# Attention pass of a macaron block: a new order of all engines, 26 waits fewer a turn

## The reference

```python
x = x + 0.5 * ffn(layernorm(x))
x = x + attn(layernorm(x))
x = x + 0.5 * ffn(layernorm(x))
```

```python
q, k, v = x @ Wq, x @ Wk, x @ Wv            # q and k then have length 1 in each head
alpha, beta = sigmoid(x @ Wa + ba), sigmoid(x @ Wb + bb)
state = alpha * state + outer(k, beta * (v - k @ state))    # token by token, 32x32 a head
y = q @ state
out = (rmsnorm(y, g_norm) * silu(x @ Wg)) @ Wo
```

## Time and profile before

| | us |
|---|---|
| median of 3 runs | 2782.89 |
| lowest and highest | 2769.9, 2797.73 |
| the profiled execution | 2779.95 |
| its span on the core | 2777.7 |
| TensorE busy | 2591.8 (93%) |
| VectorE, ACT, GpSimd busy | 1857.1, 1043.4, 1326.3 |

### The profile page before, as it was taken

How to read it: one execution, slowest core, us unless ns; L and a number is a source line. 1 busy time by engine, 2 the same in 40 slices (tenths; PEclk the granted TensorE clock), 3 DMA queues, 4 the chain that set the end, 5 groups by cost and what they waited for, 6 DMA issues and landing times.

```text
span 2777.7 us, 117151 instructions
## 1 busy us (share of the span) xinstructions
PE 2591.8 (93%) x51052; PEld 1871.6 (67%) x51052; DVE 1857.1 (67%) x5306; ACT 1043.4 (38%) x1962; POOL 1326.3 (48%) x1767
## 2 busy tenths in 40 slices
PE   7999779999999999999999999999999999999768
PEld 6788456666666667766666667776666666776544
DVE  7778456766666767666666677666676667766726
ACT  5777323333333333333333333333333333333220
POOL 2222345554545555555555555555555455555510
PEclk9999999999999999999999999999999999999968
DMA  7342122222222222222222222222222222222178
GB/s 238 104 152 85 24 66 54 62 62 65 65 65 65 64 58 64 57 66 65 57 61 65 65 65 62 65 65 60 54 61 59 65 65 65 65 65 61 54 256 317
DMA packets 365965, 224.78 MB, mean 81 GB/s; under 512 B 277584, under 2 KB 294032, under 8 KB 365456
## 3 DMA queue, kind: packets, MB, share of 16 engines
q1 hardware_dynamic: 356240, 200.51, 25.8%
q10 hardware_dynamic: 9216, 16.78, 1.6%
HBM read 125.49 MB, written 74.97 MB: 72 GB/s over the span
## 4 chain that ended last, share of the span: by engine, by line
PE 84%; DVE 8%; issue 4%; ACT 1%; DMA 1%; POOL 1%; SPq 1%; DVEq 0%; ACTq 0%; POOLq 0%
PE psum L849 24%; PE psum L906 8%; PE psum L1048 8%; PE psum L1029 5%; PE psum L970 5%; PE psum L946 4%; PE psum L1069 4%; PE psum L1009 3%; PE psum L1016 3%; PE psum L690 3%; PE psum L753 3%; PE psum L989 2%; PE psum L836 1%; PE psum L927 1%; PE psum L1089 1%
## 5 line engine op out<-in xcount | busy, mean ns | idle before, releaser
L849 PE MATMUL psum<-w_all,xnT 128*128 128x512 f32 (+2 forms) x2048 | 740.2, 500 | 1.4 <-issue 0.7
L2020 POOL TENSOR_TENSOR sm<-sm,half 128x1 f32<-128x1 f32 (+1 forms) x384 | 530.1, 1381 | 247.0 <-ACT sm L1715 231.0
L849 PEld LDWEIGHTS psum<-w_all,xnT 128*128 128x128 f32 x2048 | 369.0, 191 | 201.8 <-issue 158.2
L2585 DVE TENSOR_TENSOR blk<-blk 128x30 f32<-128x30 f32 (+14 forms) x960 | 327.8, 341 | 33.0
L2583 DVE TENSOR_TENSOR blk<-blk 128x30 f32<-128x30 f32 (+14 forms) x960 | 318.2, 331 | 40.0 <-issue 14.3
L2052 POOL TENSOR_SCALAR sm<-sm 128x1 f32<-128x1 f32 x64 | 14.8, 231 | 625.3 <-DVE sm L2490 625.3
L906 PEld LDWEIGHTS psum<-xnT,w_all 128*128 128x128 f32 x2048 | 256.0, 197 | 42.1 <-issue 34.8
L906 PE MATMUL psum<-xnT,w_all 128*128 128x128 f32 x2048 | 277.2, 285 | 1.5 <-DVE pk L2570 1.5
L1048 PE MATMUL psum<-w_out,gate 128*128 128x512 f32 x512 | 258.4, 618 | 3.0 <-issue 2.0
L1029 PEld LDWEIGHTS psum<-qg,st 32*32 32x32 f32 x8192 | 133.6, 109 | 130.0 <-DVE st L2602 64.7
L2602 DVE STREAM_TRANSPOSE st<-psum 128x128 f32<-128x128 f32 x256 | 81.0, 316 | 189.8 <-PE psum L1029 188.6
(11 more groups left out here) (278 smaller groups left out, 4719.1 us busy)
## 6 DMA issues: line engine op xcount, KB each, us to landing
blk<-n_scratch SPq DMA_DIRECT2D x64, 512.0 KB, 4.4
xin<-in_L_attn_x_dram SPq DMA_DIRECT2D x96, 256.0 KB, 3.1
n_scratch<-nn SPq DMA_DIRECT2D x64, 256.0 KB, 3.4
xh<-xc SPq DMA_DIRECT2D x64, 256.0 KB, 2.3
e_scratch<-blk SPq DMA_DIRECT2D x32, 512.0 KB, 2.8
E<-e_scratch SPq DMA_DIRECT2D x64, 256.0 KB, 3.9
x_scratch<-xh SPq DMA_DIRECT2D x62, 256.0 KB, 2.2
rxn<-in_L_attn_x_dram SPq DMA_DIRECT2D x32, 256.0 KB, 2.9
```

The costliest lines, as they stand in the source:

```text
L849: last = mm(dst, xnT[b][:, k * P:(k + 1) * P], w_all[:, k * WK + at:k * WK + at + n], start=(k == 0), stop=(k == KC - 1))
L2020: return g.tensor_tensor(dst, a, half[:, 0:n], ALU.pow)
L2585: ins = tt(Y[:, 0:rows, s_ + 1:CH], Y[:, 0:rows, s_ + 1:CH], o, ALU.add)
```

## The change

The order of all five engines in the attention pass is another; so are the PSUM banks. Waits that another wait implies are left out (many `free` and `wait_ge` lines), on TensorE 828 waiting instructions in all: a turn now has 1527 weight loads, 1527 matmuls and 18 waits, 3072 instructions. The arithmetic is the same.

A turn of TensorE now begins with apply_uw(r, 0), which stood in the turn before as apply_uw(q, 0). The cut of a turn in the functions is thus another, and the functions of b = 0 that bore the argument q there bear r here.

```diff
-        va_at = [banks(1, 1), banks(4, 1)]
+        va_at = [banks(1, 1), banks(5, 1)]
...
-        cum_at = banks(1, 1)[:, 0:8 * H]
+        cum_at = banks(6, 1)[:, 0:8 * H]
         aT_at = banks(4, 1)[:, 0:P]
-        slot_at = banks(1, 1)
+        slot_at = banks(2, 1)
...
             def ffn(n):
                 pe.wait_ge(at_in, 16 * n)
-                free((n - 2, (T["qg"][1], nth(n - 2, 0))), (n - 1, (T["pt"][0], nth(n - 1, 0))))
-                free((n - 2, (T["qg"][1], nth(n - 2, 1))), (n - 1, (S["kn"], both(n - 1, 1))))
+                free((n - 2, (T["qg"][1], nth(n - 2, 1))), (n - 1, (T["pt"][0], nth(n - 1, 0))))
+                free((n - 3, (S["slc"], n - 3)), (n - 2, (S["x2"], both(n - 2, 0))), (n - 1, (S["x1"], both(n - 1, 1))))
...
             def cum(n):
-                pe.wait_ge(S["la"], n)
-                free((n - 2, (S["slc"], n - 2)), (n - 1, (S["x2"], both(n - 1, 0))), (n, (S["va"], both(n, 0))))
+                free((n - 1, (S["ysq"], both(n - 1, 0))), (n, (S["kn"], both(n, 0))))
...
                 if piece == 0:
                     pe.wait_ge(e_in[b], 16 * n)
-                    pe.wait_ge(S["va"], both(n, b))
-                    pe.wait_ge(S["vb"], both(n, b))
-                    pe.wait_ge(S["kp"], both(n, b))
...
             def step_sp(o, p, q, r, s):
                 store_second(r, 0)
                 hold(q, 0)
+                load_alpha(o)
                 store_second(r, 1)
-                load_first(p, 1)
+                load_first(o, 0)
                 store_alpha(s)
                 hold(q, 1)
                 inverse_out(q)
-                load_alpha(o)
+                load_first(o, 1)
                 inverse_in(q, 0)
                 inverse_in(q, 1)
-                load_first(o, 0)
```

More of the change, by code:

```diff
@@ L1091, in alpha_T @@
             def alpha_T(n):
-                pe.wait_ge(S["al"], both(n + NT, 1))
-                free((n + 3, (S["xnT"], both(n + 3, 0))), (n + 2, (T["pt"][1], nth(n + 2, 1))), (n, (S["top"], both(n + NT, 0))))
                 tr(aT_at, alpha[:, :], ident[:, :]).then_inc(aT_ps, 1)
             def last_pe():
+                apply_uw(NT - 2, 0, 0)
+                apply_uw(NT - 2, 0, 1)
+                apply_uw(NT - 2, 0, 2)
+                apply_uw(NT - 2, 0, 3)
+                proj_va(NT - 1, 1, 0)
+                apply_gy(NT - 2, 0, 0)
+                proj_va(NT - 1, 1, 1)
+                proj_k(NT - 1, 1, 0)
+                proj_k(NT - 1, 1, 1)
+                proj_k(NT - 1, 1, 2)
+                proj_k(NT - 1, 1, 3)
+                apply_gy(NT - 2, 0, 1)
+                gram(NT - 1, 0, 0)
+                apply_gy(NT - 2, 0, 2)
+                gram(NT - 1, 0, 1)
+                apply_gy(NT - 2, 0, 3)
+                proj_q(NT - 1, 1, 0)
+                proj_q(NT - 1, 1, 1)
+                proj_q(NT - 1, 1, 2)
+                proj_q(NT - 1, 1, 3)
+                chain(NT - 2, 0, 0)
+                dec(NT - 1, 0)
                 chain(NT - 2, 0, 1)
-                dec(NT - 1, 0)
+                gram(NT - 1, 0, 2)
                 chain(NT - 2, 0, 2)
+                dec(NT - 1, 1)
+                gram(NT - 1, 0, 3)
+                logits(NT - 3, 1)
                 chain(NT - 2, 0, 3)
-                gram(NT - 1, 0, 2)
-                gram(NT - 1, 0, 3)
-                dec(NT - 1, 1)
-                out_proj(NT - 2, 0, 0)
                 gram(NT - 1, 1, 0)
@@ L1333, in first_pe @@
                 gram(1, 1, 3)
+                cum(1)
                 proj_g(1, 1, 0)
                 proj_g(1, 1, 1)
+                proj_g(1, 0, 0)
+                ffn(2)
                 proj_g(1, 1, 2)
-                cum(1)
-                ffn(2)
-                proj_g(1, 0, 0)
                 proj_g(1, 0, 1)
@@ L1470, in first_pe @@
-                proj_q(3, 1, 2)
-                proj_q(3, 1, 3)
-                chain(2, 0, 0)
-                gram(3, 0, 0)
-                gram(3, 0, 1)
-            def step_pe(o, p, q, r, s):
+                proj_va(3, 0, 1)
+                qe_T(2, 0, 1)
+            def step_pe(o, p, q, r, s):
+                apply_uw(r, 0, 0)
+                apply_uw(r, 0, 1)
+                apply_uw(r, 0, 2)
+                apply_uw(r, 0, 3)
+                proj_va(q, 1, 0)
+                apply_gy(r, 0, 0)
+                proj_va(q, 1, 1)
+                proj_k(q, 1, 0)
+                proj_k(q, 1, 1)
+                proj_k(q, 1, 2)
+                proj_k(q, 1, 3)
+                apply_gy(r, 0, 1)
+                gram(q, 0, 0)
+                apply_gy(r, 0, 2)
+                gram(q, 0, 1)
+                apply_gy(r, 0, 3)
+                proj_q(q, 1, 0)
+                proj_q(q, 1, 1)
+                proj_q(q, 1, 2)
+                proj_q(q, 1, 3)
+                chain(r, 0, 0)
+                dec(q, 0)
@@ L1477, in step_pe @@
                 chain(r, 0, 1)
-                dec(q, 0)
+                gram(q, 0, 2)
                 chain(r, 0, 2)
+                dec(q, 1)
+                gram(q, 0, 3)
+                logits(s, 1)
                 chain(r, 0, 3)
-                gram(q, 0, 2)
-                gram(q, 0, 3)
-                dec(q, 1)
-                out_proj(r, 0, 0)
                 gram(q, 1, 0)
@@ L1565, in step_pe @@
-                proj_q(p, 1, 1)
-                proj_q(p, 1, 2)
-                proj_q(p, 1, 3)
-                chain(q, 0, 0)
-                gram(p, 0, 0)
-                gram(p, 0, 1)
+                proj_va(p, 0, 1)
+                qe_T(q, 0, 1)
             first_pe()
```

890 lines of the change are left out of this document (411 added, 479 removed).

## The result

The changed kernel takes 2711.4 us (median of 4 runs, 2706.17 to 2713.64) against 2779.59 for the kernel before in the same comparison: ratio 0.9739, 95% interval 0.9708 to 0.9769. It is **faster by 2.6%**; the forecast was 2791 us, no change. Its profiled execution took 2713.64 us.

What follows compares the result with a forecast made beforehand. TensorE, losing time at borders of 256-instruction groups, was taken as the bound. Work 68.8, waits 0.5, borders 3.4 and 0.2 made 72.9 us a turn against 72.6, +8 us over 28 turns: 2791 us, range 2725 to 2835.

Steps and rivals of the forecast that it cites:

- The picture: TensorE's program comes in groups of 256 instructions; one run through too fast makes it wait at the border, 2.2 us a turn before.
- The first rival: TensorE's queue passes borders ahead of the array, so fixed borders cost little: 70.1 to 71 us a turn, 2713 to 2738, chance 0.30.
- I take 3.5 us from border to border as what the fetch allows: TensorE's program fetch: a group of 256 run in under 3.5 us loses the difference at its end.
- Lost: 3.5 - 1.4 = **2.1 us**, every turn: Borders in apply_gy(r, 0, 1) and (r, 0, 2): 1.4 us of work between them, so 2.1 us of issue wait each turn.
- 1.0 us in gram(q, 1): Border in the middle of gram(q, 1), 2.5 us after the one in gram(q, 0, 3): 1.0 us lost.
- Work: 68.8 forecast: TensorE's matmul time a turn: 68.5 us before plus 0.3, the same matmuls being run.
- one visit more to the small matmuls: TensorE going from 128x128 to 32x32 matmuls and back: 14 visits a turn in place of 13, 0.3 us each.
- Waits: 0.5 forecast: TensorE's waits a turn: 0.1 for chain steps of b = 0, 0.15 for query sums, 0.2 for the inverse's load, rounded to 0.5.
- The 26 wait instructions that are left out cost nothing: Implied waits left out on TensorE: worth 0 to 0.4 us a turn, taken as 0.
- Clock: 0.2 forecast: Last term of the forecast's sum for a turn, 0.2 us; its derivation is not in the text given.
- First and last turns: First and last turns of the pass, laid out anew in the same way: left at nothing.
- Turns all of one length, within 0.3 us, are the part I am surest of: Sign to look for in the profile after: every turn of the attention pass equally long within 0.3 us.

Runs made afterwards that it cites:

- e2: Changed kernel with 18 wait instructions more a turn, all at one place in proj_k(p,0,0), so the borders move by 18 a turn: 2837.7 us, ratio 1.018.
- e5: Changed kernel with 86 wait instructions run once ahead of the pass, moving its fixed borders to a bad place (245 in place of 75): 2881.9 us, ratio 1.034.
- e6: e4 with 114 wait instructions ahead of the pass, so its first fixed border stands at 250 in place of 108: 2860.7 us, ratio 1.025.
- e9: Changed kernel with proj_k(q, 1) and proj_va(q, 1, 1) moved ahead of apply_gy(r, 0, 0), leaving 32x32 work before the border at 843: 2770.2 us, ratio 0.995.
- e3: Changed kernel with one implied wait added on apply_gy(r, 0, 1) and the at_in wait moved from ffn to proj_g(q, 1, 1), 3073 instructions a turn: 2734.8 us.
- e4: Kernel before, its order and PSUM places kept, without 26 implied wait instructions a turn, so 3072 and still borders: 2729.4 us, ratio 0.978.
- e8: Changed kernel with 4 wait instructions ahead of the pass, so its borders stand 4 instructions earlier in a turn: 2711.4 us, ratio 0.972.

## Why the prediction was wrong

**The picture was right.** The program comes in groups of 256; the borders moved by 26 a turn before and stand still after; the average turn before lost 2.2 us to them. All of that holds, and e2, e5 and e6 show that these borders are the largest lever in this kernel, up to 5 us a turn either way. The first rival, that the queue passes the border ahead of the array while proj_k runs, was written down with the right place, 2713 to 2738 us, and 0.30. It is what happened at that border, where the fetch starts 2.2 us ahead and no idle time is left: a turn takes 70.6 us where it said 70.1 to 71. The measured 2711.4 us is 2 under its range, since 10 to 11 us of the gain are at the pass's end, which neither it nor the forecast counted.

**The step that failed: "I take 3.5 us from border to border as what the fetch allows"**, and with it "Lost: 3.5 - 1.4 = **2.1 us**, every turn" and 1.0 us in gram(q, 1). I had read it at two borders in the midst of 32x32 work, and there it holds: e9, with 32x32 work ahead, loses up to 2.1 us at just the border forecast. It isn't a distance between borders, though. As I read the traces, which show a fetch's start and end alone, two things set the moment: when the fetch is asked for, and that it must have landed. Take the late borders of all the traces, those with over 0.25 us of idle time (370, in nine kernels): they were passed 1.4 us (the median; 1.3 to 1.5 for the middle half) after the end of the fetch before. The fetch started up to 3.2 us ahead of its border behind slow work (e3) and up to 1.1 us after it behind 32x32 work (e9), and the same two borders came 1.38 to 1.42 us apart in e3, without loss, and 3.04 to 3.74 in e9. The changed kernel's 12 borders lose some 0.4 us in all, not 3.4. The idle time at them is 0.04 us a turn; the rest is the border in ffn (2891), which shows as longer matmuls: from the first of ffn's four to the chain behind them it is 1.06 us in e5, which has no border there, and 1.06 to 1.95, 1.46 on the mean, in the changed kernel.

What should have decided for the rival? The evidence against it was one border "19 records behind proj_g", whose successor lost 0.9. The border ahead of it had already cost 0.66 us, and the fetch behind that one ended only at 1439.6, 1.45 us ahead of the border in question: perhaps the sequencer had no instructions yet to run ahead into, which is my reading and was not tested. One row against a whole account, from a stretch already disturbed, weighed more than it should. The changed kernel's border at 2635 is its like, 37 instructions into apply_gy behind proj_g and passed 1.4 us after the fetch before it: there too the next fetch starts late, 0.8 to 1.7 us behind the border. Slow work just ahead isn't enough for a lead. That the group must have been there while that work ran fits both places but wasn't tried, and what else the lead takes stays open (at 1355, 20 instructions behind proj_q, it is 0.6 us).

**Work: 68.8 forecast, some 69.8 measured** (70.6 less 0.43 of waits and some 0.4 at borders). The forecast's 0.3 us for one visit more to the small matmuls was too small a term: against e4, the old order at a good place, the work took 1.0 us more, 69.7 against 68.7. From start to start of each matmul, without idle time, over 25 turns, the more is 0.25 us in the logits, 0.2 in proj_k, proj_q and proj_v, 0.16 in dec, 0.13 in apply_uw, and some 0.1 each in the chain, hidden, proj_g and the transpose of alpha; gram takes 0.18 less. Several of these now stand singly among other work; that this is the reason isn't shown. This error ran against the other one, which is why the gain is 2.0 us a turn and not 3.

**Waits: 0.5 forecast, 0.43 measured**, but others. The inverse's load, the query sums and the chain steps of b = 0 cost nothing; the two logits, which I hadn't named, cost it all.

**"The 26 wait instructions that are left out cost nothing"**: right, by the good turns before and in e4, 70.43 and 70.44 us. After seeing the result I held this for the wrong step, and e3 showed that it was not.

**Clock: 0.2 forecast, nothing measured**: no run shows that term, and the granted clock is 1.00 over the 25 turns.

**First and last turns "at nothing"**: from ffn of the last block to the last transpose of alpha it is 172.4 us before and 161.0 after. The sum by what was measured: 31 turns, from ffn of the first block to ffn of the last, take 2226.0 us before and 2165.6 after, 60.4 less; 11.4 at the end; the profiled run of the changed kernel came to the pass 4.5 us later, and took 0.6 more behind it. That makes the 66.7 us by which the span fell.

**"Turns all of one length, within 0.3 us, are the part I am surest of"**: they no longer drift, but they are 70.0 to 71.5 us long. The border in ffn alone gives up to 0.9 of that.

## What to carry to other kernels

Where an engine runs thousands of short instructions, number them and see whether its stalls that "waited for nothing" stand at equal distances. Here all 367 stood at one place of 256 or just behind it, in nine of the eleven traces. 86 instructions ahead of the loop cost 170 us (e5), and a turn of 3090 instructions in place of 3072 cost 126 us (e2), while the new order brought nothing inside a turn (e4). Make the turn a whole number of groups, then shift it, and measure each place: in the new order only some 20 of 256 were good (e2). At one pair of borders 1.4 us apart, slow instructions just ahead of the first made them free (changed kernel, e3, e8), and without these they cost 1.8 us a turn (e9). And don't turn two observed distances into a rule before asking what starts the clock: here late borders came 1.4 us after the end of the fetch before, at no fixed distance from the last border.

## What was unexpected of the hardware

- 86 wait instructions that run once, ahead of the pass, made the kernel 6% slower (2711.4 to 2881.9 us), by moving the borders.
- At the border in apply_gy(r, 0, 1), behind the 24 slow instructions of proj_k, the fetch starts 1.6 to 3.2 us ahead of the border, 20 to 46 instructions before it (changed kernel, e3, e8); with 32x32 matmuls there instead, 0.8 to 1.1 us after it (e9).
- The sequencer passed a wait 4.7 us ahead of the matmul behind it (e3).
- The 370 late borders were passed 1.4 us (the median) after the end of the fetch before. The transfer itself took 0.9 to 1.4 us in nine of ten fetches of the changed kernel between 600 and 2500 us, 1.6 at most.
- Wait instructions whose semaphores were already reached cost nothing that could be measured (70.43 us a turn with 26 more in the kernel before, 70.44 without them in e4, at good places), and the one in e3 held no fetch back: it started 2.4 to 3.2 us ahead of the border.
- The same code loses some 0.4 us a turn at its 12 borders in the good place (changed kernel), and in the bad place of e5 3.3 us of 75.7 in issue waits alone.
